# A decoder layer on one core: write and read weights of the memory multiplied once, reads taken by tokens

## The reference, cut to what matters

```
v  = out @ w_write.T                       # 256 x 256
wk = out shifted by one token
reads[t] = sum over s of  gamma^(t-1-s) * (out[t] . wk[s]) * v[s],   s up to t
memory   = out + 0.1 * (reads @ w_read.T)   # 256 x 256
```

## Time and profile before

| | us |
|---|---|
| median of three runs (3520.11 to 3524.64) | 3522.89 |
| span of the profiled execution | 3546.8 |
| PE busy in it | 2817.5 (79%) |
| DVE busy | 2358.7 (67%) |
| ACT busy | 1928.5 (54%) |
| POOL busy | 1775.1 (50%) |

### The profile page before, as it was taken

The page is one execution under the profiler, slowest core; times in us unless marked ns, Lnnn a source line. Parts: engine busy times, 40 slices in busy tenths (PEclk is TensorE's granted clock), DMA queues, the critical chain, the costliest instruction groups (busy, mean ns, idle before and its releaser), DMA issues.

```text
span 3546.8 us, 46325 instructions
## 1 busy us (share of the span) xinstructions
PE 2817.5 (79%) x15402; PEld 2084.2 (59%) x15403; DVE 2358.7 (67%) x3266; ACT 1928.5 (54%) x3239; POOL 1775.1 (50%) x1888
## 2 busy tenths in 40 slices
PE   3888788788887995788788788887996898999910
PEld 1666566666675653666566666675656665766600
DVE  3888988988882444888988988882444332333347
ACT  4877877887781324877887887771331111111100
POOL 1777767777781001777767777781100123222261
PEclk8998999999999896998999999999995799999955
DMA  3110111111111000011111111111102023122131
GB/s 107 31 36 32 34 36 34 34 36 41 40 44 55 28 9 25 31 37 32 35 34 34 34 37 39 40 46 54 36 1 86 33 79 132 49 77 78 50 96 55
DMA packets 101822, 163.32 MB, mean 46 GB/s; under 512 B 16610, under 2 KB 55778, under 8 KB 101634
## 3 DMA queue, kind: packets, MB, share of 16 engines
q1 hardware_dynamic: 80242, 109.94, 9.8%
q0 software_dynamic: 18064, 49.21, 4.1%
q10 hardware_dynamic: 3328, 1.76, 0.2%
HBM read 127.01 MB, written 24.38 MB: 43 GB/s over the span
## 4 chain that ended last, share of the span: by engine, by line
PE 42%; DVE 23%; ACT 13%; issue 11%; DMA 9%; POOL 1%; SPq 0%; another core or an unknown queue 0%; POOLq 0%; DVEq 0%; ACTq 0%
PE psD L1083 14%; DVE arena L1614 9%; PE psD L1181 6%; PE psA L1200 5%; ACT arena L931 4%; DMA write_w_sb<-x_dram,read_w_sb 4%; DMA write_w_sb<-write_w_sb 3%; ACT arena L921 3%; PE psD L1412 3%; DMA read_w_sb<-arena 2%; PE psD L1283 2%; PE psA L1083 2%; PE psA L1258 2%; PE psA L1190 2%; PE psD L1304 2%
## 5 line engine op out<-in xcount | busy, mean ns | idle before, releaser
L720 POOL TENSOR_TENSOR arena<-arena 128x512 f32<-128x512 f32 x1024 | 1154.2, 1154 | 17.8 <-DVE arena L1614 7.4
L1181 PE MATMUL psD<-ident,arena 128*128 128x128 f32 x4096 | 686.7, 293 | 344.4 <-DVE arena L1614 318.3
L1181 PEld LDWEIGHTS psD<-ident,arena 128*128 128x128 f32 x4096 | 482.3, 148 | 605.2 <-DVE arena L1614 375.8
L931 ACT ACTIVATE arena<-arena,negA 128x512 f32<-128x512 f32 x1024 | 719.2, 711 | 26.4 <-DVE arena L1614 25.7
L1614 DVE TENSOR_TENSOR_SCAN arena<-arena,carry,psD 128x512 f32<-128x512 f32 x512 | 641.9, 1269 | 83.3 <-PE psA L1200 75.2
L1614 DVE TENSOR_TENSOR_SCAN arena<-arena,psD 128x512 f32<-128x512 f32 x512 | 612.9, 1208 | 93.4 <-PE psA L1200 75.6
L1200 PE MATMUL psA<-ident,arena 128*128 128x128 f32 x4096 | 645.1, 283 | 0.0
L921 ACT ACTIVATE arena<-arena,bc 128x512 f32<-128x512 f32 x768 | 546.0, 711 | 118.3 <-PE psD L1181 117.6
L1200 PEld LDWEIGHTS psA<-ident,arena 128*128 128x128 f32 x4096 | 510.1, 148 | 2.1 <-issue 2.1
L704 POOL TENSOR_SCALAR arena<-arena,bc 128x512 f32<-128x512 f32 x256 | 180.8, 707 | 460.7 <-PE psD L1181 390.7
L1083 PE MATMUL psD<-arena 128*128 128x512 f32 (+4 forms) x776 | 336.1, 568 | 45.9 <-POOL strip L664 31.1
(11 more groups left out here) (230 smaller groups left out, 3840.8 us busy)
## 6 DMA issues: line engine op xcount, KB each, us to landing
arena<-c_dram SPq DMA_DIRECT2D x256, 256.0 KB, 3.1
arena<-in_W POOLq DMA_DIRECT2D x16, 1024.0 KB, 7.4
write_w_sb<-write_w_sb SPq DMA_DIRECT2D x72, 128.0 KB, 2.0
ys_dram<-arena POOLq DMA_DIRECT2D x70, 128.0 KB, 2.0
arena<-in_x SPq DMA_DIRECT2D x8, 1024.0 KB, 7.2
o_dram<-arena SPq DMA_DIRECT2D x32, 128.0 KB, 1.7
arena<-o_dram SPq DMA_DIRECT2D x4, 1024.0 KB, 5.4
x_dram<-arena SPq DMA_DIRECT2D x4, 1024.0 KB, 9.5
```

Source lines behind the costliest of these rows:

```text
L720: pool.tensor_tensor(h_ring[:, c % H_SLOTS, :], h_ring[:, c % H_SLOTS, :], c_rows[:, v % C_SLOTS, :], ALU.mult).then_inc(c_weighed, 1)
L931: act.activation(da_ring[:, c % DA_SLOTS, :], dt[:, i % 2, f, :], ACT.Exp, scale=negA[:, f, n:n + 1]).then_inc(da_ready, 1)
L1181: mm = pe.transpose(psD[:, c % FILL_BANKS, j * P:(j + 1) * P], g[:, (c // KI) % 2, j, c % KI * P:(c % KI + 1) * P], ident[:, :])
```

## The change

The product of the two weight matrices is made in the set-up: PE turns `write_w_sb`, DVE copies the turned matrix into a free piece of the scan ring (`write_T`), PE multiplies it by `read_w_sb`, and DVE writes the result over `write_w_sb`. `SETUP_D` grows from 4 to 8 jobs. In each batch `v` then already holds `out` times both matrices; the reads are summed with slices of `sm_flat` as the stationary operand and `v_sb` as the moving one, so that they come out by tokens in the `rp` banks. The `rT` jobs, their drains and the products with `read_w_sb` go. `MEM_S` is ordered by halves, and a token tile waits only for the mask that it needs last.

```diff
-    SEQ_A = [("oT", 2 * KD), ("v", TT // 2), ("rT", 2 * KD),
+    SEQ_A = [("oT", 2 * KD), ("v", TT // 2),
              ("xaT", 2 * KD), ("qT", 2 * KD), ("probs", 3 * TT)]
-    MEM_S = [(i, h) for i in range(TT) for h in range(2) if (h + 1) * JT > i]
+    MEM_S = [(i, h) for h in range(2) for i in range((h + 1) * JT)]
...
-    SETUP_D = 4
+    SETUP_D = 8
...
-        rT, xaT, qT, attT = (carve(KD * T).rearrange("p (k t) -> p k t", k=KD) for _ in range(4))
+        xaT, qT, attT = (carve(KD * T).rearrange("p (k t) -> p k t", k=KD) for _ in range(3))
...
+        write_T = h_ring[:, 0, :].rearrange("p (k f) -> p k f", k=KD)
...
-                    turned(b, "rT", rT, halves_first=False)
...
+            for m in range(KD):
+                claim_d(KD + B // 2 + m)
+                for k in range(KD):
+                    mm = pe.transpose(psD[:, m, k * P:(k + 1) * P], write_w_sb[:, k, m * P:(m + 1) * P], ident[:, :])
+                mm.then_inc(dve_full, 1)
+            pe.wait_ge(dve_drained, 2 * KD + B // 2 + RING)
+            for m in range(KD):
+                claim_d(2 * KD + B // 2 + m)
+                product(psD[:, KD + m, 0:D], [(write_T[:, k, m * P:(m + 1) * P], read_w_sb[:, k, :]) for k in range(KD)])\
+                    .then_inc(dve_full, 1)
...
-                    pe.wait_ge(dve_drained, job_d(b, "mem", len(MEM_S)) + RING)
-                    for j in range(2 * KD):
-                        k, half = j // 2, j % 2
-                        claim_a(job_a(b, "rT", j))
-                        tiles = [i for i in range(TT) if (i, half) in MEM_S]
-                        for i in tiles:
-                            lo, hi = max(P * i, half * HALF), (half + 1) * HALF
-                            at0 = sm_first[(i, half)]
-                            mm = pe.matmul(psA[:, bank_a("rT", j), lo - half * HALF:HALF], v_sb[:, i, k * P:(k + 1) * P],
-                                           sm_flat[:, at0:at0 + hi - lo], start=i == 0, stop=i == tiles[-1])
-                        mm.then_inc(act_full, 1)
-                    pe.wait_ge(act_drained, job_a(b, "rT", 2 * KD) + RING)
                     for j in range(TT // 2):
                         claim_d(job_d(b, "rp", j))
-                        token_rows(bank_d("rp", j), psD, 2 * j, rT, read_w_sb, KD).then_inc(dve_full, 1)
+                        for t in (2 * j, 2 * j + 1):
+                            half = t // JT
+                            pe.wait_ge(dve_drained, job_d(b, "mem", MEM_S.index((t, half))) + 1 + RING)
+                            at0 = [sm_first[(i, half)] + P * t - max(P * i, half * HALF) for i in range(t + 1)]
+                            mm = product(psD[:, bank_d("rp", j), t % 2 * D:(t % 2 + 1) * D],
+                                         [(sm_flat[:, at0[i]:at0[i] + P], v_sb[:, i, :]) for i in range(t + 1)])
+                        mm.then_inc(dve_full, 1)
...
+            for m in range(KD):
+                dve.wait_ge(dve_full, KD + B // 2 + m + 1)
+                dve.tensor_copy(write_T[:, m, :], psD[:, m, 0:D]).then_inc(dve_drained, 1)
+            for m in range(KD):
+                dve.wait_ge(dve_full, 2 * KD + B // 2 + m + 1)
+                dve.tensor_copy(write_w_sb[:, m, :], psD[:, KD + m, 0:D]).then_inc(dve_drained, 1)
```

## The result

The changed kernel took 3470.48 us, the median of four executions that lie far apart (3461.55, 3465.39, 3475.57, 3492.62); the kernel before, now with a fourth execution, took 3521.5 (3518.81 to 3524.64). The ratio is 0.9868, with an interval from 0.9834 to 0.9903: 51 us, where 30.6 were forecast with a range of 3484 to 3504. The direction was right, the size too small and the range wrong.

A forecast was written before the change was run, and what follows sets the result against it. The chain of waits lay on PE almost without a break through the first batch's memory. 34.1 us spared in four batches less 3.5 of set-up gave 30.6, so 3522.9 - 30.6 = 3492.3 us, range 3484 to 3504.

The forecast's parts named there:

- The fixed work: Memory stage of each batch: 24.06 us removed, 15.54 us of reads added, 8.52 us spared, 34.1 us for four.
- the running rate: Reads behind `mem`: 72 records at 0.2158 us, as in a running stream of `v`, 15.54 us; with the start 0.2241, 16.13.
- The rule of the Trainium skill: Rival for the reads: weight loads not hidden, 0.403 us a record, 23 us slower, 3546; chance 0.02.
- Waits: Reads in each batch: waits for masks and banks cost nothing; one left in force would cost 0.43 us a batch.
- `base`: POOL's last `base` pass in the second batch ends 9.8 us before the first add wants it, so it costs nothing.
- mask order: `mem` products of each batch: ordering masks by halves costs PE nothing, as the 12 shapes stay the same.
- The set-up: Ahead of the first scan loop: added transposes, copies and products start the loop 3.5 us later, once; 3.3 to 5.0 kept.
- "given back" rival: Half the gain lost through clock shifts in unchanged stages or late `base` in two batches: 3505 to 3511; chance 0.09.
- what unchanged stages do by chance of clock and phase: Stages outside the change, such as `v` and the scan loops: some 5 us either way, giving 3487 to 3501.
- a rival for the reads: Clock falls in the reads: 0.319 us a record, 23.0 us a batch, gain only 1 us, 3522; chance 0.03.
- The profiled span: Whole kernel: median of runs 23.9 us below the profiled 3546.8 us; the same saving taken from 3522.9.

The follow-up runs named there:

- all_masks: The changed kernel with one wait for all twelve masks ahead of the reads of each batch; 3474.37 us, ratio 0.9876.
- late_one: The changed kernel with one product 128x256 of constants, read by nobody, ahead of the reads of each batch; 3485.74 us, ratio 0.9891.
- after_again: The changed kernel, unchanged, profiled a second time and timed in five rounds; 3486.45 us, ratio 0.991.
- after_warm2: The changed kernel with unread products of constants in PE's pauses, those of second batches ahead of the wait for ACT's drains of `oT`; 3455.91 us, ratio 0.9824.
- after_warm3: after_warm2 with 12 more unread products ahead of the 64 counting products and one between each 16; 3460.46 us, ratio 0.9826.

## Why the prediction was wrong

**The fixed work was right.** Forecast 8.52 us a batch, measured 8.45 (31.11 - 15.50 = 15.61 for the reads, forecast 15.54). The choice of the running rate, 0.2158 us a record, over the stage's mean held where the reads follow `mem` without a stop; with the stop of all_masks they took 15.85 us instead of 15.61. The rule of the Trainium skill, "TensorE: Matmul & The Clock Gate", section "The mechanism", that a weight load overlaps a matmul in flight only when the row groups differ, is contradicted again if it is read alone: 13.27 us of loads lie inside the 15.61. The same section also lets a load into the background weight buffer go ahead of the matmuls in flight, and with that the trace agrees; the prediction left this out. Waits, `base` and mask order cost nothing, as said. The set-up was forecast at 3.5 and its steps took 3.2, beside a random 1.0 in the products ahead of them. One bound does not follow: 2 x 8.5 us lost end at 3509, not at the 3511 of the "given back" rival.

**The step that failed is the term "what unchanged stages do by chance of clock and phase: some 5 us either way".** I read it from differences inside one profile of before, and treated it as noise around a mean. Three things were missed. First, the clock was already low in every batch of that profile at `wo` (9.3 to 9.8 us where 7.19 is possible, clock 0.73 to 0.77) and behind `x2` (0.53); there it could hardly lose and had 4 x 2.4 + 9.4 = 19 us to win, against some 2 us that `v` lost, so the term was nearly one-sided. The earlier trace rows showed a clock of 0.70 in one stretch, and I used it only as a rival for the reads; the question to ask was where else PE runs slow, and whether a shift of the stages could end that. Second, the four batches have the same schedule and often win or lose together: in each profile of before and of the changed kernel as it stands `wo` is slow in all four or in none, though all_masks has two of each and late_one one near 7.2 and three slow. Errors that I added as if independent came as one step of 20 us and more. Third, the first loop varies more than the 3.6 us between the two loops of one profile: with the same work it ended at 1093.30 us in all_masks (clock 0.96) and at 1105.02 in late_one (0.93). The "given back" rival had the right cause and only the wrong sign.

**How much is the kernel's.** The four executions of the result held two near 3463, one at 3476 and one at 3493; the five of after_again none under 3481. Whether the first median fell into the range was thus a matter of which executions were drawn: 3486.45 lies inside 3484 to 3504, 3470.48 and 3470.63 outside. Over 13 the changed kernel is 37 to 40 us faster than before. By subtraction 7 to 10 of that are clock that it gets more often than the kernel before, which in 51 executions never left its 16 us. Why the changed kernel can have `wo` at the full clock and the old one does not, is not settled: the rows show the clock at 1.2 GHz behind the products of the attention with `vblk` in one and not in the other, with the same instructions ahead of it. What was shown is that the same program goes both ways, and that in profiles with PE's pauses filled the four batches differ by the fixed work and 1.4 us.

**The profiled span.** That the 23.9 us above the median lay outside the stages concerned was assumed, and was true: they are in the final adds (136.79 against 112.47).

## What to carry to other kernels

Price the work that a change takes off the path by the running rate of the same shape of record; where the records followed without a stop, that held here to 0.1 us in 15.5. Then list the stretches where TensorE runs below its full clock: each is room that a shift may win or lose, all repeats together, and it belongs in the range with its sign. Take such a result from several executions and several profiles, compare them stage by stage, and fill PE's pauses in both kernels if need be, before explaining a few tenths of a per cent.

## What the runs showed of the hardware

- One program, unchanged, took 3461.55 to 3492.62 us in 13 executions, with a mean granted clock from 0.928 to 0.915; the kernel before stayed within 3509.8 to 3526.0 in 51, at 0.922 to 0.914.
- The same 32 records of `wo` took 7.19 us at a clock of 1.00 in four of four batches in one execution of that program, and 9.03 to 9.13 at 0.78 to 0.79 in four of four in another.
- The clock can stay at 1.2 GHz with PE's records back to back: the 128 counting records took 27.59 us, PE busy in 27.57 of them by its records, at a clock of 0.50 (after_warm2). With products 128x512 ahead of them and between them they ran at 1.00, 0.119 us each in the last quarter instead of 0.2155 (after_warm3).
- Products that nobody reads, put where PE waits, made both kernels faster: the kernel before by 31 us (0.9898 [0.9874, 0.9921]), and the changed one to 0.9824 [0.9808, 0.984].
- Weight loads of full 128x128 float32 weights lay beside the products: 13.27 us of loads in the 15.61 us of 72 records with new weights each.
